# Attention written out without a loop, its sums copied two exponentials sooner; in the scan, u loaded two states sooner and sums three steps behind

## The reference, cut to what matters

```python
# layer 0, over 8 sequences of 1024 tokens, D = 256, N = 16 states per channel
decay = jnp.exp(dt[..., None] * A)
inp = (dt * x)[..., None] * Bm[:, :, None, :]          # u = dt * x
def step(s, td):
    dec, ip, c = td
    s = dec * s + ip
    y = jnp.einsum('bdn,bn->bd', s, c)
    return (s, y)
y = y + D_skip * x
...
# layer 1, gate branch: 16 heads, 8 columns each for scores and values
scores = jnp.einsum('bhsk,bhtk->bhst', Q[..., :KPH], K) / math.sqrt(KPH)
attn = jax.nn.softmax(scores, axis=-1)
ao = jnp.einsum('bhst,bhtv->bhsv', attn, V)
```

## Time and profile before

| | us |
|---|---|
| Median of 3 runs | 4421.24 (4420.6 to 4423.72) |
| Profiled execution | 4448.79 |
| Its span, first to last instruction | 4447.1 |

### The profile page before, as it was taken

One profiled execution on the slowest core, in us unless ns is written; L12 is line 12 of the kernel. 1 busy time (PEld: TensorE's weight loads), 2 busy tenths in 40 slices (PEclk: granted clock), 3 DMA queues, 4 the chain that ended last, 5 costly groups with the idle time before them and its releaser, 6 DMA issues. The chain is left out here.

```text
span 4447.1 us, 70510 instructions
## 1 busy us (share of the span) xinstructions
PE 3601.8 (81%) x19727; PEld 2105.8 (47%) x19728; DVE 3339.8 (75%) x4247; ACT 2313.7 (52%) x4132; POOL 1343.6 (30%) x873
## 2 busy tenths in 40 slices
PE   8978888888549868778699999999999995449960
PEld 3445555555335567777533333333333333349960
DVE  8959888889764456645688888888888864558768
ACT  6755555554764423220047777777777772113323
POOL 4458888888003332410100000000000002644530
PEclk9989999999779979889779999999999996579985
DMA  6654444443858832347412223222222203323249
GB/s 215 251 192 162 157 156 157 155 155 121 271 187 192 185 93 71 94 108 211 121 30 49 70 49 69 49 61 57 55 64 55 64 8 104 119 62 92 89 135 299
DMA packets 534112, 537.39 MB, mean 121 GB/s; under 512 B 84720, under 2 KB 439792, under 8 KB 533664
## 3 DMA queue, kind: packets, MB, share of 16 engines
q1 hardware_dynamic: 507328, 475.20, 36.6%
q0 software_dynamic: 13952, 37.74, 2.5%
q10 hardware_dynamic: 12544, 20.98, 1.8%
HBM read 317.41 MB, written 215.19 MB: 120 GB/s over the span
## 5 line engine op out<-in xcount | busy, mean ns | idle before, releaser
L2126 DVE TENSOR_REDUCE at_top<-at_psM 128x1 f32<-128x1024 f32 x1024 | 1205.8, 1219 | 211.3 <-PE at_psM L1975 210.2
L2085 ACT ACTIVATE at_probs<-at_psS 128x512 f32<-128x512 f32 x2048 | 1068.9, 603 | 338.4 <-PE at_psS L2001 327.8
L2001 PE MATMUL at_psS<-at_q,at_k 64*128 64x512 f32 x2048 | 806.7, 471 | 18.0 <-ACT at_probs L2085 8.2
L568 POOL TENSOR_TENSOR sc_prod<-sc_state,sc_c_row 128x1024 f32<-128x1024 f32 x256 | 707.4, 2782 | 153.0 <-DVE sc_state L717 141.7
L1975 PE MATMUL at_psM<-at_k,at_q 62*128 62x512 f32 x2048 | 683.4, 448 | 51.3 <-DMA at_vraw<-scratch_vf 22.3
L717 DVE TENSOR_TENSOR_SCAN sc_state<-sc_dec,sc_psI 128x1024 f32<-128x1024 f32 x256 | 579.2, 2280 | 77.0 <-PE sc_psI L638 45.5
L1975 PEld LDWEIGHTS at_psM<-at_k,at_q 62*128 62x128 f32 x2048 | 322.8, 192 | 601.8 <-DVE at_top L2126 534.9
L2014 PE MATMUL at_psV<-at_probs,at_v 128*32 128x512 f32 x4096 | 553.7, 613 | 33.5 <-ACT at_sums L2090 31.4
L649 PE MATMUL sc_psY<-sc_prod,sc_ident 128*128 128x512 f32 x1024 | 481.1, 610 | 40.8 <-DVE sc_y L703 35.5
L599 ACT ACTIVATE sc_dec<-sc_dt,sc_a_exp 128x1024 f32<-128x1024 f32 x256 | 293.6, 1148 | 328.2 <-DVE sc_state L717 325.1
L2001 PEld LDWEIGHTS at_psS<-at_q,at_k 64*128 64x128 f32 x2048 | 341.4, 186 | 221.6 <-ACT at_probs L2085 213.8
(11 more groups left out here) (394 smaller groups left out, 5011.9 us busy)
## 6 DMA issues: line engine op xcount, KB each, us to landing
sc_c_row<-scratch_bc SPq DMA_DIRECT2D x128, 512.0 KB
scratch_xs<-at_zeros SPq DMA_DIRECT2D x140, 264.0 KB, 4.8
sc_b_row<-scratch_bc SPq DMA_DIRECT2D x64, 512.0 KB, 5.2
ec_y<-scratch_ys SPq DMA_DIRECT2D x32, 512.0 KB, 6.7
ex_x<-scratch_xs SPq DMA_DIRECT2D x39, 264.0 KB, 2.9
si_x<-in_x SPq DMA_DIRECT2D x16, 512.0 KB, 4.4
scratch_xn<-si_xn SPq DMA_DIRECT2D x16, 512.0 KB, 5.2
scratch_x_t<-si_xT SPq DMA_DIRECT2D x16, 512.0 KB, 5.8
```

The costliest lines, as they stand in the source:

```text
L568: pool.tensor_tensor(prod[:, (n * H + h) % 8, :], state[slot][:], c_row[n % ROWS][:], ALU.mult).then_inc(prod_ready, 1)
L2001: pe.matmul(psS[v % 3][:], rows_of(k4[j], h, 0, GROUP)[:, c * P:(c + 1) * P], rows_of(q4[j], h, 0, GROUP)[:, half * TILE:(half + 1) * TILE ...
L2085: act.activation(probs[:, slot(j, v), :], psS[v % 3][:], ACT.Exp).then_inc(act_done, 1)
L2126: dve.tensor_reduce(top[j % 2][:, h, c:c + 1], psM[t % 2][:], AX.X, ALU.max, negate=True).then_inc(maxed, 1)
```

## The change

Four edits. In the scan `LAG` goes from 2 to 3. Also in the scan, u of the next batch is loaded at n = 2 instead of n = 4, on a semaphore of its own that `turn` and `mix` wait for; dt and x stay where they were, and at the scan's start both halves of u are loaded first. In attention the streams of TensorE, ScalarE and VectorE are written out for all 8 sequences, with constants in place of registers; SyncE and GpSimd keep their loops. And `OPEN` goes from 6 to 4, `MIDDLE` from entry 38 to entry 36.

```diff
@@ ssm_scan
-    LAG = 2
+    LAG = 3
...
+                def load_u(b, k):
+                    for h in two:
+                        sp.dma_start(u[k][h][:], unit("u_t", b, h)).then_inc(u_loaded[k], 16)
+
                 def load(b, k):
                     for h in two:
-                        sp.dma_start(u[k][h][:], unit("u_t", b, h)).then_inc(loaded[k], 16)
                         sp.dma_start(dt[k][h][:], unit("dt_t", b, h)).then_inc(loaded[k], 16)
                         sp.dma_start(x[k][h][:], unit("x_t", b, h)).then_inc(loaded[k], 16)
...
                         if place < 3 and n == 4:
                             load(b + 1, 1 - k)
+                        if place < 3 and n == 2:
+                            load_u(b + 1, 1 - k)
...
+                load_u(0, 0)
                 load(0, 0)
...
-                            pe.wait_ge(loaded[1 - k], (b + 1 - (1 - k)) * 48 + 96)
+                            pe.wait_ge(u_loaded[1 - k], (b + 1 - (1 - k)) * 16 + 32)
                             pe.wait_ge(state_ready, b * PER + (TURN - 1 + h))
                             turn(b + 1, 1 - k, h, psI[h])
...
-                pe.wait_ge(loaded[0], 96)
+                pe.wait_ge(u_loaded[0], 32)
                 turn(0, 0, 0, psI[1])
...
                 def mix(b, k, own, place):
                     d, h = MIXED.index(own // H), own % H
-                    dve.wait_ge(loaded[k], (b - k) * 48 + 96)
+                    dve.wait_ge(u_loaded[k], (b - k) * 16 + 32)
@@ attention
-    OPEN = 6
-    MIDDLE = at_slot[38]
+    OPEN = 4
+    MIDDLE = at_slot[36]
...
-                with pe.Fori(0, B - 1) as b:
-                    sequence(b, False)
-                sequence(B - 1, True)
+                for b in range(B):
+                    sequence(b, b == B - 1)
...
-                with act.Fori(0, B - 1) as b:
-                    sequence(b, False)
-                sequence(B - 1, True)
+                for b in range(B):
+                    sequence(b, b == B - 1)
...
-                for j in range(NQ):
-                    unit(j, j)
-                with dve.Fori(1, B) as b:
-                    for j in range(NQ):
-                        unit(b * NQ + j, j)
+                for u in range(UNITS):
+                    unit(u, u % NQ)
```

More of the change, by code:

```diff
@@ L472, in ssm_scan @@
         a_made, a_exp_made = m.sem("a_made"), m.sem("a_exp_made")
-        loaded, c_loaded = [m.sem(f"loaded{k}") for k in two], [m.sem(f"c_loaded{k}") for k in range(ROWS)]
+        u_loaded, loaded = ([m.sem(f"{n}loaded{k}") for k in two] for n in ("u_", ""))
+        c_loaded = [m.sem(f"c_loaded{k}") for k in range(ROWS)]
         b_turned, b_ready, u_turned, uT_ready = m.sem("b_turned"), m.sem("b_ready"), m.sem("u_turned"), m.sem("uT_ready")
@@ L593, in batch @@
                             if own == 0:
-                                act.wait_ge(loaded[k], (b - k) * 48 + 96)
+                                act.wait_ge(loaded[k], (b - k) * 32 + 64)
                             if own in (TURN + 2, TURN + 3) and place < 3:
@@ L698, in output @@
                 def output(b, k, h):
-                    dve.wait_ge(loaded[k], (b - k) * 48 + 96)
+                    dve.wait_ge(loaded[k], (b - k) * 32 + 64)
                     dve.wait_ge(y_added, (b + 1) * PER - (1 - h))
```

## The result

| | median | lowest to highest | runs |
|---|---|---|---|
| before | 4420.92 us | 4419.52 to 4423.72 | 4 |
| changed | 4306.07 us | 4303.44 to 4310.76 | 4 |

The ratio is 0.9741 [0.9729, 0.9753]: 2.6% faster, 115 us, where 130 were forecast. 4306 lies inside the range and 15 us above the predicted 4291.

What follows compares the result with a forecast made beforehand. No engine is always busy: the scan is bound by VectorE's waits, attention by a repeating 2.61 us cycle plus interruptions. Terms of 29.0 + 16.6 + 1.8 + 45.7 + 37.1 = 130.2 us off 4421.2 gave 4291 us, range 4272 to 4330.

Steps and rivals of the forecast that it cites:

- starts of batches: Scan, seven later batches: with LAG 3 VectorE's waits at steps 4 and 5 go, 29.0 us (15 to 29).
- turn of u: Scan: u loaded two states sooner ends TensorE's DMA wait and shortens VectorE's wait before `mix`, 16.6 us (0 to 25.1).
- scan's start: Start of the scan: with u loaded first, the turn's wait for six loads goes, 1.8 us (0 to 1.8).
- attention's loops: Attention: written-out streams save six turns back and the register instructions, 45.7 us (27 to 46).
- copies of the sums: Attention: copies moved behind the fourth exponential fit ScalarE's idle time, 0.58 us each, 37.1 us (10 to 41).
- B: Scan: u sooner brings nothing, DMAs at their limit or another wait last; 18.4 us less gained, 4309; chance 0.09.
- C: Attention: the 0.68 us a unit belongs to the loads, not registers; 18.5 us less gained, 4310; chance 0.09.
- A: Attention: the copy is not hidden and pushes the next exponentials by 0.49 us; 27 less gained, 4318; chance 0.12.
- D: Attention: straight code stalls for instruction fetches, 4.45 us each, 249 us in all; slower, 4540; chance 0.04.

Runs made afterwards that it cites:

- Experiment 3: The kernel before with only LAG raised from 2 to 3 in the scan: 4388.29 us, ratio 0.9925.
- experiment 5: The kernel before with only ScalarE's attention stream written out, TensorE and VectorE keeping their loop: 4421.47 us beside 4445.95, one run.
- experiment 1: The kernel before with only attention's TensorE, ScalarE and VectorE streams written out: 4375.26 us beside 4419.38, ratio 0.9895.
- Experiment 7: The changed kernel with LAG 2 in the first batch up to step 12, LAG 3 from there on: 4335.32 us beside 4445.95, one run.
- experiment 8: The changed kernel with the scan's loop written out too, on all five engines: 4323.43 us beside 4445.95, ratio 0.9729.
- experiments 2: The kernel before, loops kept, with only OPEN 4 and MIDDLE 36: 4390.54 us, ratio 0.9932.
- experiment 4: The kernel before with only the earlier u on its own semaphore, LAG 2: 4404.13 us, ratio 0.9967.

## Why the prediction was right, and where its sum was off

| term | forecast | whole change | |
|---|---|---|---|
| starts of batches | 29.0 | 28.3 | right in sum: waits 30.3, `mix` of step 6 held -1.9 |
| turn of u | 16.6 | 10.5 | the term that was mis-sized |
| scan's start | 1.8 | 1.0 | small |
| attention's loops | 45.7 | 45.1 | right (45.1 alone) |
| copies of the sums | 37.1 | 34.2 | 0.09 a copy pushed, not 0.06 |
| first batch | 0 | -2.2 | not foreseen |
| behind the loop's turns in the scan | 0 | -2.1 | may be chance |
| step 8 of two batches | 0 | -2.8 | not foreseen |
| between scan and attention | 0 | 3.2 | varies by itself |
| sum | 130.2 | 115.2 | |

- **Starts of batches.** The waits at steps 4 and 5 went as forecast, clock included. From step 3 to step 6 the later batches take 9.3 to 9.5 us, from 12.5 to 14.2. Experiment 3 has it alone. But "in the rest of a batch ... nothing is added" failed twice: `mix` of step 6 now falls on GpSimd's product (1.52 us for 1.21, seven times, 1.9 us), and step 8 is below. That the sum is within 0.7 of the forecast is in part luck.
- **Turn of u.** Half right. The DMA wait went whole, and the wait left for the turned u is 1.2 us against 1.4. Wrong was to take `mix` at its 1.23 us of the earlier trace rows. That row began at 418.35, when GpSimd's product had just ended (at 418.09 in that trace); moved ahead, `mix` falls on the product. At 1.14 us that is 7 or 8 us in seven batches, less 1.4 for the shorter waits: the size of the miss, 6.1. The row that showed it was in the prediction and was read wrongly: `mix` of 3.02 us at 741.02 was put down to TensorE's lower level, though VectorE's scans take 2.26 to 2.29 us in every trace, at either level of that clock. In that trace GpSimd's product ran from 740.60 to 742.96, and `mix` ended 1.08 behind it.
- **Attention's loops.** The length of a unit in the last, already straight sequence was the right yardstick: 43.23 forecast, 43.26 measured. Both halves were shown apart, registers in experiment 5, turns in what it left. By the branch of 108 ns that the Trainium skill has (Advanced Engine Details and Errata, Control Flow Timing) the loops would be worth some 20 us, an estimate; the run has 45.1, so the page's figure is no price of a whole turn back.
- **Copies.** The mechanism is right (next exponential 0.49 behind the copy). The allowance for the semaphore was 0.03 too small, 64 times: 2 of the 2.9 us. The rest is that the two cycles with a copy took 3.21 and 3.26 us in straight code (experiment 1), not 3.25 both.
- **First batch.** I said that "in the rest of a batch each `add` only asks for an older product; nothing is added". In the first batch it does add something: the `adds` were what kept TensorE at work between two inputs. Experiment 7 shows it, with the reserve that the loss came once with LAG 2 as well.
- **Loop's turns and step 8.** I held the two waits of the earlier trace rows, 2.05 and 3.61, for fixed. They are 3.8 and 3.9 in the changed kernel. And LAG 3 more than doubled TensorE's idle time ahead of step 8's input (2.26 us for 0.98), where the clock then fell in two batches. The forecast put that at nothing. That the turns go once there is no loop, experiment 8 shows; that a fall of the clock a batch stays, it shows too. Why it falls at one idle time and not at another, no run settles.
- **Rivals.** The time alone, 4306, stands nearer to B (4309) and C (4310) than to the forecast. The runs tell them apart: A, C and D have experiments 2, 5 and 1 against them, and B experiment 4, in which the earlier u alone gains 15 us of medians. The 3.2 us of the third stage went the forecast's way by chance; without them 18 us of the forecast would be missing, still inside the range.

## What to carry to other kernels

A wait removed is worth what the next thing allows, and that thing may be another engine's instruction that merely runs at the same time: before an instruction is moved, look what GpSimd does in the place where it will land. A delay line (here the lag of the adds) is also what keeps TensorE busy between two urgent inputs, so look at the first turn, where there is nothing old to fill it with, and at every later place where one more step of lag lengthens an idle time. Where one sequence is already written out, its period beside the loop's gives the price of the loop to within a us.

## What the runs showed of the chip

- VectorE's product of two SBUF operands, issued while GpSimd's runs, takes 2.37 us instead of 1.23 and ends 1.1 us behind it; VectorE's scan, which has one operand in PSUM, takes its 2.28 us beside GpSimd's product.
- TensorE fell to its 1.2 GHz level behind single idle times of 2.10, 2.18 and 3.16 us in a scan that otherwise stands at 1.00, and did not fall behind others of the same length (2.10, 2.25, 3.15); in straight code the fall recurs at one place of each batch, and filling that place moved it to another.
- One loop turn back cost 4.45 us in attention, with two packets of instructions 3.0 to 3.4 us apart beside it; a register instruction ahead of ScalarE's wait cost 0.08 to 0.09 us each time on the path. Straight code of eight sequences cost nothing that shows: one of the two queues that bring instructions had 117 packets and 1.92 MB over the whole kernel, against 136 and 2.23 with the loop:

```profile
q8 instruction: 117, 1.92, 0.2%
```

- Two chips differ by some 28 us in one unchanged stretch of 720 us, and by no more than unchanged code varies in the others.
